# Sums by relation in two steps: 32-column masks per chunk, then seven quads per tile

## The reference, cut to what matters

```
h = relu(layernorm(x))
for l in range(3):                       # relational layers
    xr  = einsum('nd,rde->rne', h, W_rel[l])
    agg = segment_sum(xr[edge_type, src], dst, 6250)
    h   = relu(agg + h @ W_root[l] + bias[l])
x = x + h
h = relu(layernorm(x))                   # attention layer
h = h @ Wv + bv;  q = h @ wq + bq;  k = h @ wk + bk
c = leaky_relu(q[src] + k[dst], 0.2)
out = segment_sum(h[src] * segment_softmax(c, dst), dst, 6250)
x = x + out
```

## Time and profile before

| | us |
|---|---|
| median of 3 runs | 5282.95 (5263.98 to 5283.96) |
| span of the profiled execution | 5218.2 |
| layer 0, from POOL's first gather to its last | 1169.9 |
| layer 1 | 1155.6 |
| layer 2 | 1129.9 |
| attention layer | 1268.1 |

### The profile page before, as it was taken

How to read it: one execution, slowest core, us unless ns; L and a number is a source line. 1 busy time by engine, 2 the same in 40 slices (tenths; PEclk the granted TensorE clock), 3 DMA queues, 4 the chain that set the end, 5 groups by cost and what they waited for, 6 DMA issues and landing times.

```text
span 5218.2 us, 55702 instructions
## 1 busy us (share of the span) xinstructions
PE 3531.3 (68%) x12674; PEld 2474.9 (47%) x12674; DVE 1648.4 (32%) x4423; ACT 2203.5 (42%) x6033; POOL 3049.7 (58%) x3295
## 2 busy tenths in 40 slices
PE   9986877788785777677775544545454666566666
PEld 4444554555553445445453333334333555455555
DVE  4533333334341222222221111111113444444444
ACT  2332443344432434343343333333334555555555
POOL 1135666666655666666664666666664566556664
PEclk9997988898887888888887777767677878878788
DMA  6554555555543444344443333333332333333332
GB/s 212 193 199 130 184 186 176 178 186 192 183 169 126 132 133 139 125 136 138 131 137 95 103 103 103 103 101 105 102 102 77 93 98 96 95 95 97 98 96 75
DMA packets 240046, 681.43 MB, mean 131 GB/s; under 512 B 60188, under 2 KB 111988, under 8 KB 215028
## 3 DMA queue, kind: packets, MB, share of 16 engines
q0 software_dynamic: 152400, 419.03, 27.6%
q10 hardware_dynamic: 57240, 186.43, 9.7%
q1 hardware_dynamic: 30092, 72.34, 3.8%
HBM read 501.99 MB, written 175.58 MB: 130 GB/s over the span
## 4 chain that ended last, share of the span: by engine, by line
PE 31%; another core or an unknown queue 28%; ACT 14%; issue 14%; DVE 9%; DVEq 2%; ACTq 1%; DMA 0%; SPq 0%; POOL 0%
PE bank L1546 13%; PE sum_ps L1632 9%; ACT masks L1357 4%; ACT masks L1451 4%; PE sum_ps L1758 3%; DVE root L810 3%; PE bank L1708 2%; DVEq L809 2%; ACT wide L1428 2%; PE bank L1714 2%; ACT masks L1364 1%; PE turn_ps L1531 1%; ACT stage L1467 1%; ACT wide L1461 1%
## 5 line engine op out<-in xcount | busy, mean ns | idle before, releaser
L592 POOL DMA_INDIRECT ring<-table,code x2361 | 2233.3, 946 | 1357.2 <-issue 661.9
L1632 PE MATMUL sum_ps<-ring,masks 128*128 x5292 | 1403.2, 423 | 199.2 <-issue 196.9
L1632 PEld LDWEIGHTS sum_ps<-ring,masks 128*128 128x128 f32 x5292 | 1126.6, 216 | 453.9 <-issue 271.2
L1546 PE MATMUL bank<-wide,xT 128*128 128x512 f32 (+1 forms) x2744 | 1125.2, 564 | 7.9 <-issue 6.3
L592 POOL DMA_INDIRECT ring<-h_table,code x787 | 746.6, 949 | 519.3 <-SPq L732 275.0
L1357 ACT ACTIVATE masks<-node_row,local 128x128 f32<-128x128 f32 x2646 | 788.5, 388 | 27.8 <-issue 13.7
L1546 PEld LDWEIGHTS bank<-wide,xT 128*128 128x128 f32 x2744 | 515.6, 190 | 563.6 <-issue 552.0
L1255 ACT ACTIVATE xT<-turn_ps 128x256 f32<-128x256 f32 x196 | 75.5, 385 | 1429.0 <-remote 587.4
L1758 PE MATMUL sum_ps<-ring,stage 128*128 x1764 | 492.7, 426 | 76.8 <-ACT stage L1467 48.7
L1264 ACT COPY stage<-bank 128x512 f32<-128x512 f32 x441 | 243.9, 582 | 590.0 <-remote 353.6
L810 DVE SCALAR_TENSOR_TENSOR root<-bank,loops,root 128x256 f32<-128x256 f32 x686 | 331.0, 483 | 369.5 <-ACT stage L1264 179.5
(11 more groups left out here) (216 smaller groups left out, 2504.3 us busy)
## 6 DMA issues: line engine op xcount, KB each, us to landing
table<-stage ACTq DMA_DIRECT2D x96, 1024.0 KB
back<-table ACTq DMA_DIRECT2D x49, 1024.0 KB
table<-stage SPq DMA_DIRECT2D x48, 1024.0 KB
ring<-table,code POOLq DMA_INDIRECT x2361
ring<-h_table,code POOLq DMA_INDIRECT x787
h_table<-stage ACTq DMA_DIRECT2D x49, 130.0 KB
back<-h_table ACTq DMA_DIRECT2D x49, 130.0 KB
features<-xT SPq DMA_DIRECT2D x49, 128.0 KB, 4.0
```

The source lines that it names most:

```text
L592: pool.indirect_dma_start(slot(c % RING, width), None, table, bass.IndirectOffsetOnAxis(ap=code[:, c:c + 1], axis=0)).then_inc(landed[n % ...
L1546: last = nc.tensor.matmul(bank[q][:, 0:width], xT[:, b, k, :], weights[:, k, 512 * q:512 * q + width], start=(k == 0), stop=(k == K - 1))
L1632: last = nc.tensor.matmul(sum_ps[b][:, 0:D], masks[:, b, s, :], at_offset(slots[s]), start=(s == 0 and l > 0), stop=(s == SLOTS - 1))
```

## The change

**Windows.** Destinations are sorted, so the 128 edges of a chunk end in few neighbouring nodes. Each chunk is now summed once, by a mask of 128x32 (edge by node relative to the chunk's least node), and the result of 32 rows by 256 columns goes to rows 32 x (c mod 4) of a PSUM bank: the four chunks of a quad fill the four groups of 32 columns of PE's array. Two quads are a pair and share a bank; ACT copies each pair to SBUF (`keep_pairs`). A chunk's place in the ring is known when the program is built.

**Quads.** A tile then adds seven matmuls of 128x128 by 256 columns over the summed quads; which seven is fixed (`first_quad`). For about two new pairs, 16 chunks, there are so 16 window matmuls and 7 quad matmuls.

**Masks.** DVE builds both kinds: 16 window masks in one operation of 128x512 (`mask_windows`), a tile's seven masks in one of 128x896 (`mask_tile`). Before the layers there are new steps that compute each edge's relative node and each quad row's node (`relative`, `spread_quads`, `keep_relative`, `name_rows`, on DVE, with 14 transposes and a matmul more on PE and some operations on POOL). If the edges of a chunk spread over more than 32 nodes, or a tile needs a chunk outside its seven quads, a flag sends the edges to the slow path that was there before.

**Ring.** In the relational layers POOL waits for the quad ten back to have been summed in its windows (`quad_done`), no longer for SP. PE waits for the landing itself. SP's relay is left for the attention layer, and SP now issues the loads and stores of the relational layers, where ACT did.

**Order.** The transform is in two parts, with half of the new windows ahead of the turn and half between the parts. Bank 4 and the turn now share one PSUM bank, as two sums do. DVE adds the first layer's self-loops in `root` in SBUF, no longer in a PSUM bank.

The core of the diff:

```diff
+    def first_quad(t):
+        middle = CH * (P * t + P / 2) / N
+        return max(0, min(round((middle - GROUP * SPAN / 2) / GROUP), GROUPS - SPAN))
...
+    def new_pairs(t):
+        pairs = range(pairs_to(t - 1), pairs_to(t))
+        half = (len(pairs) + 1) // 2
+        return pairs[:half], pairs[half:]
...
             def gather_pass(l, table, width):
                 if l:
-                    pool.wait_ge(in_order, l * GROUPS)
+                    pool.wait_ge(quad_done, l * GROUPS)
                 for n in range(GROUPS):
-                    if n >= RINGS:
-                        pool.wait_ge(released, l * RELEASES + n - RINGS + 1)
+                    if n >= RINGS and l < L:
+                        pool.wait_ge(quad_done, l * GROUPS + n - RINGS + 1)
+                    elif n >= RINGS:
+                        pool.wait_ge(released, n - RINGS + 1)
...
-                    nc.vector.scalar_tensor_tensor(root[:, i, :] if t == R - 1 else loop_ps, back[:, b, t * D:(t + 1) * D],
-                                                   loop_weight(i, t), loop_ps if t else root[:, i, :], ALU.mult, ALU.add
-                                                   ).then_inc(back_step, 1)
+                    nc.vector.scalar_tensor_tensor(root[:, i, :], back[:, b, t * D:(t + 1) * D], loop_weight(i, t),
+                                                   root[:, i, :], ALU.mult, ALU.add).then_inc(back_step, 1)
...
+            def mask_windows(l, first, end):
+                for k in range(first, end):
+                    chunks = range(CHUNKS_AT_ONCE * k, min(CHUNKS_AT_ONCE * (k + 1), CH))
+                    if l or k > 1:
+                        reused = l * GROUPS + (2 * PAIR * (k - 1) if k > 1 else 0)
+                        dve.wait_ge(quad_done, reused)
+                    shape = [P, len(chunks), WINDOW]
+                    nc.vector.tensor_tensor(window_masks(k)[:, 0:len(chunks), :],
+                                            rel_T[:, chunks[0]:chunks[-1] + 1].unsqueeze(2).to_broadcast(shape),
+                                            node_row[:, 0:WINDOW].unsqueeze(1).to_broadcast(shape), ALU.is_equal
+                                            ).then_inc(window_masked, 1)
...
             for l in range(L - 1):
                 conv_head(l)
+                first_masks(l)
                 dve.wait_ge(weights_loaded, weights_of(l + 1))
-                sum_up(l, 0, 0, 0)
-                for i in range(1, NT):
+                if l == 0:
+                    add_first_loops(0, 0, 0)
+                for i in range(NT):
                     j, b = divmod(i, 2)
...
+                    sum_up(l, i, j, b)
+                    upcoming_masks(l, i + 2)
+                    if l == 0 and i + 1 < NT:
+                        add_first_loops(i + 1, (i + 1) // 2, 1 - b)
+                    next_table(l, i, j, b)
...
+            def keep_pairs(l, pairs):
+                for p in pairs:
+                    act.wait_ge(quad_done, l * GROUPS + min(PAIR * (p + 1), GROUPS))
+                    if l or p >= SUM_RING:
+                        act.wait_ge(added, tile_added(l, tiles_of_pair(p - SUM_RING) - 1) if p >= SUM_RING
+                                    else tile_added(l, -1))
+                    width = D * (min(PAIR * (p + 1), GROUPS) - PAIR * p)
+                    nc.scalar.copy(pair_sums(p)[:, 0:width], pair_ps[p % 2][:, 0:width]).then_inc(pair_kept, 1)
...
+            def sum_windows(l, pairs):
+                for p in pairs:
+                    if l or p > 1:
+                        pe.wait_ge(pair_kept, l * NP + p - 1 if p > 1 else l * NP)
+                    for q in range(PAIR * p, min(PAIR * (p + 1), GROUPS)):
+                        k = GROUP * q // CHUNKS_AT_ONCE
+                        pe.wait_ge(window_masked, l * MASK_BATCHES + k + 1)
+                        pe.wait_ge(landed[q % RINGS], 16 * gathers_to(l, q))
+                        for c in chunks_of(q):
+                            at_row = c % GROUP * WINDOW
+                            last = nc.tensor.matmul(pair_ps[p % 2][at_row:at_row + WINDOW, q % PAIR * D:(q % PAIR + 1) * D],
+                                                    window_masks(k)[:, c % CHUNKS_AT_ONCE, :], slot(c % RING, D),
+                                                    start=True, stop=True)
+                        last.then_inc(quad_done, 1)
...
+                for s in range(SPAN):
+                    last = nc.tensor.matmul(sum_ps[b][:, 0:D], masks[:, b, s, :], quad_sums(first_quad(i) + s),
+                                            start=(s == 0 and l > 0), stop=(s == SPAN - 1))
+                last.then_inc(added, 1)
...
+                for i in range(NT + 1):
+                    early, late = new_pairs(i) if i < NT else ((), ())
+                    sum_windows(l, early)
+                    if i:
+                        j, b = divmod(i - 1, 2)
+                        turn_sum(l, j, b)
+                        transform((l + 1) * NT + i - 1, (l + 1) * USES[b] + j, b, [0, 1])
+                    sum_windows(l, late)
+                    if i:
+                        transform((l + 1) * NT + i - 1, (l + 1) * USES[b] + j, b, list(range(2, NB)))
+                    if i < NT:
+                        sum_tile(l, i, i // 2, i % 2)
```

More of the change, by code:

```diff
@@ L1369, in conv_head, with keep_bank @@
+            def keep_bank(l, use, b, q):
+                act.wait_ge(transformed[b], CREDIT + NB * use + q + 1)
+                if q == 0:
+                    act.wait_ge(stored[b], table_stored(l, b, use))
+                nc.scalar.copy(stage[:, b, 512 * q:512 * (q + 1)], bank[q][:, :]).then_inc(evacuated[q], 1)
             def conv_head(l):
@@ L1426, in lower_score @@
+            conv_head(L - 1)
+            for i in range(NT + 1):
+                early, late = new_pairs(i) if i < NT else ((), ())
+                if i:
+                    deviation(NT + i - 1)
+                keep_pairs(L - 1, early)
+                if i:
+                    j, b = divmod(i - 1, 2)
+                    relu_turned(L * USES[b] + j, b, h_ready[b], j)
+                keep_pairs(L - 1, late)
             def lower_score(c, i, b):
```

436 lines of the change are left out of this document (227 added, 209 removed).

## The result

The changed kernel took 5248.37 us (median of 12, 5238.72 to 5262.00), the kernel before 5278.94 (12, 5263.16 to 5286.29): ratio 0.9948, 95% interval 0.9937 to 0.9959. The forecast was 4807 (4745 to 5020). The gain is 31 us, not 476.

A forecast was written before the change was run, and what follows sets the result against it. POOL's gathers bound the passes, 984 us each. First stage 369.5 + 5, three passes with starts of 25.7, 15 and 15, pauses of 33, 32 and 27, attention 1268.1: 4742; with 64.8, 4807 us (4745 to 5020).

The forecast's parts named there:

- The step that failed is the first: POOL in the passes: waits of 208.0, 192.1 and 159.9 us were for ring room, which the new ring rule would free.
- The floor stays: POOL's gathers in each pass: the same 787 at 1.25 us each, 984 us a pass.
- Rival 2: Passes: waits only change their name, engines still chained tile by tile; half of 504 us stays, 5029 us; chance 0.14.
- PE per tile: PE's work a tile: 16.6, 15.6 and 9.6 us in layers 0 to 2, under POOL's 20.1, so no bound.
- 18 x 388 ns: ACT's work a tile: distances no longer computed there, put at 5.4 us saved; ACT not waited for.
- Rival 1: PE's windows: no two overlap, PE just the bound in layer 0 at 20.2 us a tile; 4840 to 4870; chance 0.09.
- the slower rival: PE's windows in layers 0 and 1: 0.88 us each with loads in the open, +639 us, 5446; chance 0.04.
- rival 3: DVE's masks and loops with two SBUF inputs stop POOL's gathers: 279 us in layer 0, 88 in others; chance 0.03.
- Start of a layer: POOL stands still while DVE wakes: 15 us each in layers 1 and 2 (bounds 0 and 30), 25.7 in layer 0.
- Between the passes: Pauses without gathers after each pass: 33, 32 and 27 us, where 49.3, 42.5 and 33.4 stood.
- First stage: New small steps on DVE, POOL and PE before the layers: 5 us more (bounds 0 and 13).
- The 64.8 us: Median of the runs less the traced span of 5218.2 us, added to the forecast span at the end.

The follow-up runs named there:

- e6: The kernel before, unchanged, run again for a trace from that chip; passes of 993.2, 984.7 and 988.5 us.
- e16: The kernel before, unchanged, timed and traced once more: 4436.96 us.
- e1: The changed kernel with only the first two of a quad's four chunks gathered in layers 1 and 2: 3720.57 us, kernel before 4432.11.
- e17: The changed kernel, unchanged, run again beside the kernel before: 4524.64 us against 4436.96.
- e7: The changed kernel with one self-loop operation a tile in layer 0 instead of eight: 4512.95 us.
- e8: The changed kernel building only 1 of 16 window masks and 1 of 7 tile masks in layers 1 and 2: 5249.99 us, kernel before 5272.97.
- e9: The changed kernel with each mask built by its own operation from one SBUF tensor and a column of scalars: 5280.54 us, kernel before 5272.97.
- e12: The changed kernel with only two of a quad's four chunks gathered in layers 1 and 2, repeated: 4256.57 us, kernel before 5256.46.
- e5: The changed kernel, unchanged, run again beside the kernel before: 4524.15 us against 4431.41, ratio 1.0209.

## Why the prediction was wrong

**The step that failed is the first**, "This is why layer 2 waits 159.9 us though PE is idle half the time", with "The floor stays". I took the excess of 186, 172 and 146 us over 1.25 us a gather for want of room in the ring. e6 and e16 show the same ring, relay and rule with 1 to 9 us of excess. At the late level, to which the first traces belong, PE's signals came late in the kernel before too (in its layer 1 the median from the end of a sum to z is 4.2 us, 0.09 in e16). Its relay waited for these signals, and the changed kernel, which has no relay in these layers, waits for them as well. No pass there went below 1.43 us a gather: the kernel before already stood at that in layer 2 (1129.9, and 1129.7 after), 26 us above it in layer 1 and 40 in layer 0, and the traces show 16.8 and 9.5 us won there. What delays the signals stays open. The attention layer's rows should have warned me: PE was no bound there either.

**Rival 2** was the right one in kind, waits that only change their name, from SPq L732 to "remote" and PE. I gave it 0.14 and half of the excess; nearly all stayed (477 of the 504 us). What I had put under it, a chain tile by tile, was not the cause: e1 ran that chain at 13.5 us a tile.

**PE per tile.** Right in direction: no bound. Windows cost 1.7 us a tile (four quads at 0.43) where I took 3.6 and allowed 1.8 to 14.1. PE's busy time a tile still came out near my 16.6, 15.6 and 9.6 (e17: 16.4, 15.9 and 9.7), which was luck: the windows were 1.9 us cheaper, and the transform took longer in places than in my rows (eight of its instructions 5.40 us at 1380.85 in e17, 3.70 at 1388.86). For ACT I wrote 18 x 388 ns beside 5.4 us; the product is 7.0, and 5.4 is its busy time (788.5 us by 147 tiles). Nothing hangs on it. The rule of the Trainium skill ("TensorE: Matmul & The Clock Gate", Part 3: Packing small matmuls) that a load overlaps only a matmul of another row group did not hold for these: their loads of 32 columns last 115 ns each on all rows, and run while matmuls of the same rows are in flight. Rival 1 and the slower rival fall with it.

**DVE and POOL.** I gave rival 3 little for two operations of 256 columns that delayed no gather; those of 512 and 896 columns, which the change adds, do, and so do the eight loops in a row in layer 0 (e7). The Trainium skill ("SBUF — State Buffer", Who interferes with whom) has it that a DVE instruction with two SBUF inputs contends with GpSimd's reads; e7, e8 and e9 agree: gathers busy 765.9 us with such masks, 745.3 and 746.0 without. Its size is 15 to 28 us a pass at the prompt level, not 88 to 279; at the late level POOL's busy time grew by 22 to 35 us and the passes did not.

**Start of a layer.** The 66.41 us of DVE were 29.6 us of waiting for the sum and then 36.8 us of a late signal of PE, no branch. The last piece of that sum, in the first trace of before:

```profile
1615.48 1.13 PE L1632 MATMUL sum_ps<-ring,masks 128*128 x4 [2.99 <-issue]
```

It ended at 1616.61, 28 us after the first gather, DVE had its branch behind it at 1587.19, and the trace records the signal at 1653.25. In e16 the sum ends 28 us after the first gather as well, and DVE, past the same branch, begins z at 1414.57, 0.2 us after it. In the changed kernel it built the first masks at once:

```profile
1414.57 0.42 DVE L1042 TENSOR_TENSOR z<-sum_ps,root 128x256 f32<-128x256 f32 x1 [29.84 <-PE sum_ps L1632]
```

```profile
1594.53 2.09 DVE L969 SCALAR_TENSOR_TENSOR masks<-row_node,node_row 128x896 f32<-128x896 f32 x2
```

I had added 15 us for each start and left 25.7 in layer 0. At the prompt level no pass of the changed kernel has such a wait; at the late level layer 1's first 125 us hold 14.1 us of waits (8.7 and 5.4).

**Between the passes** I forecast 33, 32 and 27: 33.2, 31.7 and 24.7 at the prompt level, which is close. I compared them with 49.3, 42.5 and 33.4 and booked a gain. But those were longer by late signals too; like with like the change loses 7 to 11 us there. At the late level PE is still three tiles behind when POOL ends, and the pauses are 58.1 and 56.0.

**First stage**: +5 forecast, +7.0 and +7.6 measured.

**The 64.8 us** that I added to the span is no time around an execution: the changed kernel's traced execution took 5238.72 with a span of 5237.0, and so with the others. By the same difference the traced execution of before took about 5220, an estimate; it was shorter than the timed ones.

## What to carry to other kernels

An excess over an engine's floor has a cause only when the releaser is named and its own work ends where the wait ends. Waits that end microseconds after the releaser was done are no want of room, and no edit to the order or the amount of work removed them here, other than fewer gathers. Before pricing such a wait as a gain, look for a stage that the change doesn't touch and that shows the same excess (here the attention layer), and for the same hand-over where the suspect engine rests (here after the last gather). Work moved to DVE beside a gathering POOL lengthens gathers when it reads two SBUF tensors; whether one-input operations, which took DVE longer, win in the end has to be measured, and no version here did.

## What the hardware showed that I had not expected

- The same kernel took 4431 or 5273 us, a fifth apart, on one chip in different groups of runs. Of the 790 us between the two traced spans of before, 726 lie in stretches in which POOL gathers. What makes a chip late or prompt stays open. So does what delays PE's signals: in the rows it goes with how densely gathers come (prompt at 1.75 us a gather in e12, late at 1.50 and below), not with their bytes. A rival that no run tests is the recording itself: all but the first three timed executions have a recorded span beside their time, and the traces at the late level hold 23200 to 27500 records of semaphore updates where those at the prompt level hold 55800 to 70600.
- So the verdict on the change depends on it: 0.9948 where signals are late (one group of runs), 1.0197 (1.0180 to 1.0214, e17) and 1.0209 (e5) where they are prompt. Why timed runs at the late level gained 31 us, when the two traces show 26 won in the passes, 26 lost between them and 19 more in the first stage and the attention layer, isn't settled: there is one trace of before at that level, of an execution shorter than the timed ones.
- Four 128x32 float32 windows in four column groups take 0.43 us together, about the time of one full-width matmul (0.448), with their loads hidden.
